# Pairs' layers of the later quarters: one fp32 matmul, or three fp32r terms of split x and split matrix

## The reference

```python
x = x + einsum('bct,bcd->bdt', x, W0[itok_B_1_198])
x = x + einsum('bct,bcd->bdt', x, W1[itok_B_0_7])
x = x + einsum('bct,bcd->bdt', x, W2[itok_B_0_7]) + bias[itok_B_0_7][:, :, None]
gate = x @ Wg + (x @ Ag[a]) @ Bg[a]          # 512 -> 2048, a = itok_B_0_7, rank 16
up   = x @ Wu + (x @ Au[a]) @ Bu[a]
h    = silu(gate) * up
x    = x + h @ Wd + (h @ Ad[a]) @ Bd[a]      # 2048 -> 512
```

## Time and profile before

| | before |
|---|---|
| median of three runs, and their range | 1240.14 us (1238.54 to 1240.18) |
| the profiled execution: its own time, its span | 1237.63 us, 1235.8 us |
| TensorE busy | 1227.7 us, 99% of the span |
| weight loads busy | 1029.7 us, 83% |
| VectorE busy | 957.1 us, 77% |
| ScalarE busy | 558.1 us, 45% |
| GpSimd busy | 710.7 us, 58% |
| granted TensorE clock | full (1.00) in the whole span |

### The profile page before, as it was taken

How to read it: one execution, slowest core, us unless ns; L and a number is a source line. 1 busy time by engine, 2 the same in 40 slices (tenths; PEclk the granted TensorE clock), 3 DMA queues, 4 the chain that set the end, 5 groups by cost and what they waited for, 6 DMA issues and landing times.

```text
span 1235.8 us, 18085 instructions
## 1 busy us (share of the span) xinstructions
PE 1227.7 (99%) x6190; PEld 1029.7 (83%) x6190; DVE 957.1 (77%) x1540; ACT 558.1 (45%) x1003; POOL 710.7 (58%) x598
## 2 busy tenths in 40 slices
PE   9999999999999999999999999999999999999998
PEld 8888888888888888888888888888888888888886
DVE  7887777887688777788678778777868877677775
ACT  4744445444544344454344444444534443444333
POOL 4676655558736556546864556555675554444453
PEclk9999999999999999999999999999999999999999
DMA  6866455556865455557496544546659442322323
GB/s 213 295 214 220 126 153 186 162 163 185 289 223 162 124 158 144 164 162 213 142 332 191 178 128 143 166 137 187 198 180 314 160 120 80 93 84 86 113 89 107
DMA packets 141690, 209.60 MB, mean 170 GB/s; under 512 B 44192, under 2 KB 88480, under 8 KB 141600
## 3 DMA queue, kind: packets, MB, share of 16 engines
q1 hardware_dynamic: 117696, 135.45, 34.8%
q0 software_dynamic: 23040, 71.85, 19.0%
q10 hardware_dynamic: 864, 1.15, 0.3%
HBM read 164.36 MB, written 44.04 MB: 169 GB/s over the span
## 4 chain that ended last, share of the span: by engine, by line
PE 97%; DVE 2%; issue 0%; ACT 0%; POOL 0%; DVEq 0%; POOLq 0%
PE px L1735 29%; PE pd L1735 28%; PE py L1735 14%; PE pz L1735 7%; PE pz L1752 3%; PE pv L1781 2%; PE pv L1779 2%; PE pd L2074 2%; PE py L1752 2%; PE px L1752 2%; PE pd L1762 1%; PE px L1886 1%; PE py L1886 1%; PE pd L1871 1%; PE px L1758 1%; PE pd L1904 0%
## 5 line engine op out<-in xcount | busy, mean ns | idle before, releaser
L803 POOL TENSOR_TENSOR h_lo<-g,h_hi 128x512 fp32r<-128x512 f32 x127 | 182.4, 1437 | 298.0 <-ACT h_hi L943 297.2
L766 POOL DMA_INDIRECT b_got<-b_table,idx_b x192 | 198.5, 1034 | 59.9 <-issue 49.9
L1735 PE MATMUL px<-xo_hi,wg_hi 128*128 128x512 f32 x516 | 207.2, 402 | 1.3 <-DVE wg_lo L1382 0.9
L1513 DVE TENSOR_TENSOR acc<-pd,acc 128x512 f32<-128x512 f32 x248 | 164.3, 684 | 51.6 <-PE pd L1735 51.6
L1382 DVE TENSOR_TENSOR wg_lo<-w_raw,wg_hi 128x512 fp32r<-128x512 f32 (+1 forms) x256 | 182.8, 720 | 26.5 <-ACT wg_hi L943 26.4
L1735 PE MATMUL px<-xo_hi,wg_lo 128*128 128x512 f32 x516 | 202.5, 392 | 0.0
L1735 PE MATMUL px<-xo_lo,wg_hi 128*128 128x512 f32 x516 | 201.0, 389 | 0.0
L943 ACT ACTIVATE wg_hi<-w_raw 128x512 fp32r<-128x512 f32 (+1 forms) x260 | 146.0, 570 | 121.1 <-PE py L1752 74.6
L1735 PE MATMUL pd<-wd_hi,h_hi 128*128 128x512 f32 x504 | 199.7, 396 | 0.0
L1735 PE MATMUL pd<-wd_lo,h_hi 128*128 128x512 f32 x504 | 197.9, 393 | 0.0
L1735 PE MATMUL pd<-wd_hi,h_lo 128*128 128x512 f32 x504 | 196.6, 390 | 0.0
(11 more groups left out here) (331 smaller groups left out, 2439.6 us busy)
## 6 DMA issues: line engine op xcount, KB each, us to landing
w_raw<-w_gu SPq DMA_DIRECT2D x65, 512.0 KB, 4.8
wd_raw<-w_dn SPq DMA_DIRECT2D x64, 256.0 KB, 3.5
xo_hi<-xops SPq DMA_DIRECT2D x21, 512.0 KB, 6.0
xo_lo<-xops SPq DMA_DIRECT2D x21, 512.0 KB, 7.3
acc<-x SPq DMA_DIRECT2D x8, 1024.0 KB, 6.8
ad_raw<-ad_table SPq DMA_DIRECT2D x16, 512.0 KB, 4.3
ad_table<-ad_rows_kept SPq DMA_DIRECT2D x12, 512.0 KB, 6.5
xops<-st_hi SPq DMA_DIRECT2D x24, 256.0 KB, 2.8
```

Source lines behind the costliest of these rows:

```text
L766: gp.indirect_dma_start(out=dst, out_offset=None, in_=rows_of, in_offset=bass.IndirectOffsetOnAxis(ap=rows.bitcast(U32), axis=0)).then_inc ...
L803: return gp.tensor_tensor(dst, src_raw, src_hi, ALU.subtract)
L1513: ins = dve.tensor_tensor(dst, pd[j][:, :], dst, ALU.add)
L1735: ins = pe.matmul(psum, w_parts[wi], x_parts[xi], start=(start and i == 0), stop=(stop and i == 2), skip_group_check=more)
```

## The change

The matrix and x of the pair are both split, and the layer becomes a `split_product`.

- ScalarE makes `x_hi`, a copy of 128x512 values: for the block's own pair in block 3 (behind `keep_s2`, and now it is ScalarE that waits for the load of x), and for the next pair right behind the bias addition that ends each layer (`add_bias`).
- GpSimd makes `x_lo`, a subtraction over 128x512: for pair 0 in block 3, behind `gather_pair`; for the next pair at the end of each block's work on GpSimd, behind `h_low(q, b, 1)` and ahead of `gather_ad`.
- VectorE makes three instructions over 128x128 of the one: `f_hi` in fp32r, `f_one` in fp32, and, behind a wait for the latter, `f_lo`, their difference, which now signals `f_done`. `f_hi` and `f_lo` lie in an unused part of `v`.
- TensorE waits for `f_done` and `x_lo_done` and issues three matmuls of 128x512.
- The memory set aside for GpSimd's transfer descriptors is 4096 bytes in each partition and not 8192, which is the room of `x_hi` and `x_lo`.

```diff
+        x_hi = sb("x_hi", [P, T], F32R)
+        x_lo = sb("x_lo", [P, T], F32R)
...
+        def pair_tokens(q, i):
+            return acc[:, (q + 1) % 2, PAIR_ORDER[i], :]
...
+        f_hi, f_lo = v[:, 1, WH:WH + P], v[:, 1, WH + P:2 * WH]
...
+            def x_low(q, i):
+                gp.wait_ge(x_hi_done, made(q, i))
+                low(x_lo[:, :], pair_tokens(q, i), x_hi[:, :]).then_inc(x_lo_done, 1)
...
                     gather_pair(q, i)
+                if pair_at(q, b) == 0:
+                    x_low(q, 0)
...
                     gather_own(q + 1, (*range(13, 16), *range(0, 2)))
+                if pair_at(q, b) is not None and pair_at(q, b + 1) is not None:
+                    x_low(q, pair_at(q, b + 1))
                 if ad_gather_at(q, b) is not None:
...
+            def x_high(q, i):
+                if i < 2:
+                    act.wait_ge(x_in[(q + 1) % 2][i], ((q + 1) // 2 + 1) * 16)
+                copy(x_hi[:, :], pair_tokens(q, i)).then_inc(x_hi_done, 1)
...
                 keep_s2(k)
+                if pair_at(q, b) == 0:
+                    x_high(q, 0)
...
-                    add_bias(acc[:, (q + 1) % 2, pair, :], pd[0][:, :], (q + 1) * QP + pair).then_inc(layer_add, 1)
+                    add_bias(pair_tokens(q, i), pd[0][:, :], (q + 1) * QP + pair).then_inc(layer_add, 1)
+                    if i + 1 < QP:
+                        x_high(q, i + 1)
...
+                    dve.tensor_tensor(f_hi, pd[2][:, 0:P], eb_one[:, i % 2, :], ALU.add)
                     dve.tensor_tensor(f_one[:, :], pd[2][:, 0:P], eb_one[:, i % 2, :], ALU.add
-                                      ).then_inc(f_done, 1)
+                                      ).then_inc(f_summed, 1)
+                    dve.wait_ge(f_summed, e)
+                    dve.tensor_tensor(f_lo, f_one[:, :], f_hi, ALU.subtract).then_inc(f_done, 1)
...
-                    if i < 2:
-                        pe.wait_ge(x_in[(q + 1) % 2][i], ((q + 1) // 2 + 1) * 16)
                     pe.wait_ge(f_done, made(q, i))
-                    pe.matmul(pd[0][:, :], f_one[:, :], acc[:, (q + 1) % 2, PAIR_ORDER[i], :],
-                              start=True, stop=True).then_inc(layer_mm, 1)
+                    pe.wait_ge(x_lo_done, made(q, i))
+                    split_product(pd[0][:, :], [f_hi, f_lo], [x_hi[:, :], x_lo[:, :]]
+                                  ).then_inc(layer_mm, 1)
...
-    nc = bacc.Bacc("TRN2", target_bir_lowering=False, num_devices=1, dynamic_dma_scratch_size=8192)
+    nc = bacc.Bacc("TRN2", target_bir_lowering=False, num_devices=1, dynamic_dma_scratch_size=4096)
```

More of the change, by code:

```diff
@@ L303, in cond_resid_kernel @@
         e_mm = sem("e_mm")
+        f_summed = sem("f_summed")
         f_done = sem("f_done")
+        x_hi_done = sem("x_hi_done")
+        x_lo_done = sem("x_lo_done")
         layer_mm = sem("layer_mm")
```

## The result

| | before | after |
|---|---|---|
| median of five runs each | 1238.62 us | 1244.66 us |
| range | 1238.09 to 1240.18 | 1244.38 to 1246.4 |
| ratio, with its 95% interval | | 1.0047 (1.0032 to 1.0062) |

The account below looks back on a forecast made before the run. TensorE bounds the kernel, 97% of the span. Gain -4.3, nine waits +9.5 and block 4's +1.2 give +6.4 us (bounds +3.9 and +8.3), on the median 1240.14 1246.5; 1244.0 to 1248.5 for this case, overall range 1239.5 to 1250.5.

Parts of the forecast that it names:

- TensorE's gain: At each of 24 layers, one fp32 matmul of 0.86 becomes three of 0.23: 0.18 gained each, 4.3 us in all.
- VectorE's own part: At the pair's matrix, `f_done` comes 0.82 behind the start of `f_hi`, 0.54 later than before, hidden by 0.94 in block 6.
- ScalarE's part: 24 copies of 128x512, 0.63 each, in ScalarE's idle time behind `add_bias`: cost nothing.
- The seam: Between `h_lo` and `x_low` at an odd block's end: VectorE's waiting sum stays held through both, its string 1.30 later.
- Rows 6: Trace at 127.72: two GpSimd subtractions back to back, 2.55 together, VectorE's sum ending behind the second; taken as more alike.
- Both rivals that let VectorE through at the seam: VectorE's string slips through, wait hidden, 1235.8 us, chance 0.12; or VectorE keeps the ports, `x_low` late, 1240.5, chance 0.12.
- rows 7: Trace at 159.38: VectorE's gate ends 0.54 behind the first of two GpSimd subtractions; taken as lower bound, 0.86 a block.
- The wait: Ahead of the layer in blocks 6, 8, 10: 1.06 us each, nine times, 9.5; first quarter's block 4: 1.2.
- The idle time in brackets: Sign to look for: about 0.9 to 1.0 of idle ahead of the layer's first matmul in blocks 6, 8 and 10.
- Block 4 of later quarters: Matrix made at 416.05; with the delays 418.33 for a layer at 418.40, just in time, so no wait.
- Odd blocks: Blocks 5, 7 and 9: `x_low` delays VectorE's work, but 2.63 of cover stand against 1.30 + 0.54, so no wait.
- The fourth case, slower gathers: GpSimd's gathers slower with half the descriptor memory, or a later load of x: +7 on top, about 1253 us, chance 0.10.

Follow-up runs that it names:

- experiment 1: The changed kernel without GpSimd's `x_low`, the layer's second term reading `x_hi` again; 0.9966 of the kernel before, 1236.06 against 1240.16 us.
- experiment 5: The changed kernel with `x_low` moved ahead of the first tile's `h_low`, all work kept; 0.9972 of the kernel before, 1234.96 against 1238.59 us.
- experiment 7: The changed kernel with the subtraction that makes `x_lo` replaced by a fill with zeros at the same place; 0.9966 of the kernel before, 1234.77 us.
- experiment 3: The kernel before with the matrix made in two parts by three VectorE instructions, the fp32 layer kept; 1.0005 of the kernel before, 1240.98 us.
- experiment 8: The changed kernel with `x_low` over 256 of the 512 columns, the other half zero; 0.9997 of the kernel before, 1237.78 us.
- experiment 9: The changed kernel with all of `x_low` done as two subtractions of 256 columns; 1.0027 of the kernel before, 1242.21 against 1238.29 us.
- experiment 6: The changed kernel with `x_low` moved ahead of the first `h_low` in odd blocks only; 0.9966 of the kernel before, 1235.07 us.
- experiment 4: The kernel before with 4096 and not 8192 bytes of descriptor memory, nothing else; 1.0007 of the kernel before, 1241.44 us.

## Why the prediction was right

The forecast was +6.4 us on the kernel before and 1246.5; measured are +6.0 and 1244.66. Of the 1.8 us between the two times, 1.5 is the median of before, which I took as 1240.14 and which is 1238.62 over five runs. That the medians differ by just 6.0 is in part luck: the interval allows 4.0 to 7.7, and the profiled executions differ by 0.9 in the opening alone, where nothing was forecast. What bears the prediction out is the stretch from 60 us on, +5.8 for +6.4, and the steps below.

- **TensorE's gain, 0.18 a layer.** 0.18 at each of 24 layers (experiments 1, 5 and 7), 4.3 in all. The layer is worth 3.8 reduced matmuls (0.86 / 0.227; the prediction divided by the rounded 0.23 and had 3.7); by the four passes of the Trainium skill ("FP8 and Floating Point Precision", TensorE Precision Notes), experiment 1 would have been 5.5 shorter from 60 us on, and it is 4.3.
- **VectorE's own part, 0.54 and hidden.** `f_lo` ends 0.81 behind the start of `f_hi` (155.94 to 156.75), 0.82 was forecast. Hidden: experiment 3.
- **ScalarE's part, nothing.** No engine but VectorE ends a wait ahead of a layer in the changed kernel, and experiment 1, which keeps the copies, has none.
- **The seam.** Rows 6 were the right pair to go by: 3.42 against 2.18, 1.24 where I had 1.30, since two subtractions back to back take 2.54 and not 2.60. Both rivals that let VectorE through at the seam are refuted in 9 of 9 blocks, and `x_lo` takes its plain 1.30 and not over 2.5. With half the size VectorE's first sum does get through (experiments 8 and 9), so the choice between rows 6 and rows 7 was a real one. The reason given for it (in rows 7 the first subtraction had itself waited) fits the full size only: in experiments 8 and 9 `h_lo` runs its plain 1.30 and VectorE gets in all the same.
- **The wait, 1.06 each.** Measured 1.01 in the nine blocks, and 1.14 for 1.2 in the first block 4. These two are the 0.5 between +6.4 and +5.9. The idle time in brackets, given as the sign to look for at 0.9 to 1.0, is 0.73: it starts 0.17 after the next matmul could have begun, which the prediction left out of the sign, though not out of the price.
- **Block 4 of later quarters, nothing.** `f_lo` is ready 0.29 before the layer there; I had 0.23, of which 0.16 for the way to TensorE. In the first quarter's block 3 `x_lo` is ready 0.22 before the layer; I had 0.4. For the block 3 the cover is thin enough that in experiment 6 it was used up.
- **Odd blocks, nothing.** `f_lo` has 1.49 or more to spare in them, although in block 5 VectorE's first sum of the next weights is held for 3.44 us, where it was 2.23.
- **The fourth case, slower gathers.** Experiment 4: none.

The Trainium skill ("SBUF — State Buffer", Who interferes with whom) has the exclusion between a VectorE instruction with two SBUF inputs and a GpSimd instruction that reads SBUF. Experiment 7 supports that it hangs on reading: the fill lets VectorE pass. Its order of issue the trace does not bear out at the full-size seam: by the recorded starts the sum was issued at 151.21, ahead of both `h_lo` (151.79) and `x_lo` (153.03), and ended behind both. GpSimd had a gather under way at 151.21 (150.83 to 151.77), but that doesn't explain it: the 186 sums of 128x256 in this trace that run beside gathers alone take 0.41 to 0.49. Why this one had not ended by 151.62, ahead of `h_lo`, the traces don't show.

## What to carry to other kernels

Before giving GpSimd one more elementwise instruction, look at which VectorE instruction stands next to it at that moment and how much cover its consumer has: the same 21 subtractions (the other three stand in block 3 in both) cost 10 us of waits at the end of a block, all of it at ten of them, and nothing when they stood ahead of an earlier `h_low`, where GpSimd had idle time. Two small delays share one cover: 0.54 on VectorE was free alone, and doubled the price of the other. For what a wait costs, take the distance of two starts, not the idle time in the bracket, which was 0.28 too small here each time.

## What the hardware showed that I had not expected

**Who gets through at a seam changes with the second instruction's size, and not by size alone.** A VectorE sum held by a GpSimd subtraction of 128x512 stays held through a second one of 128x512 (3.42 us, 9 of 9), and gets through ahead of a second one of 128x256 (2.24 us, 9 of 9 in each of two kernels). The half-size subtraction takes 1.01 in such a crossing in experiment 8, where the shortest one of experiment 9 takes 0.73, so VectorE isn't the only one that pays.

It is no rule of size in general. In each of the eleven kernels, the one before included, VectorE gets in at 24 other seams, ahead of instructions that are not small: at 12 between an `h_lo` and the 128x768 subtraction, and at 12 between that one and the next `h_lo`. At the first kind the `h_lo` had itself taken 1.61 in place of 1.30. Where the first ran its plain 1.30 and the second was of 128x512 (`x_lo` or a down weight), VectorE was held through both, in 15 of 15 cases of the changed kernel and in 3 of 3 before; but once, in the first block 3 of the changed kernel, it got in behind a plain 1.30 and ahead of the 128x512 subtraction for `ad`. No one rule for all of these came out.

**The opening varies, the rest hardly does.** From 60 us on, three kernels without a wait at a layer are 4.33, 4.40 and 4.31 shorter than before. In the first 48 us, in which no edit but the single fill at the start of experiment 8 moves an instruction, ten profiled executions (the changed kernel and nine experiments) lie between 0.0 and 4.0 us behind the one of before. Each is one execution of another kernel; that it is chance and no effect of an edit is my reading, and the 23 runs of the kernel before beside experiments 5 to 8, from 1237.68 to 1241.49, spread as much. These are windows of 10 us with each engine's busy time, TensorE first, then the granted clock; the kernel before:

```profile
10.00:20.00 10.00, 10.00 (x76) 8.75 (x75) 7.82 (x23) 2.50 (x6) 5.83 (x6) 1.00 0.76 257
20.00:30.00 10.00, 10.00 (x56) 7.18 (x55) 9.55 (x37) 8.98 (x17) 3.31 (x2) 1.00 0.73 252
```

And that of experiment 4, whose opening is 4.0 longer:

```profile
10.00:20.00 10.00, 8.38 (x74) 8.14 (x73) 5.40 (x11) 1.33 (x4) 5.95 (x6) 1.00 0.77 274
20.00:30.00 10.00, 10.00 (x38) 5.79 (x39) 8.53 (x44) 6.15 (x10) 1.26 (x2) 0.83 0.77 242
```

TensorE was idle for 1.6 us of the first window, waiting for VectorE once (1.6 us), and for 3.4 us of the next window, from 20.17 on, it was granted the lower of its two levels, 1.2 in place of 2.4 GHz. Experiment 3 has the same picture (8.38 busy, then a clock of 0.84); experiment 1 had as long a pause (8.34 busy) and kept its full clock, with an opening 2.1 longer. What makes the pause come in one execution and not in another I did not look into. It means that with one execution of each, a difference of 4 us in span says nothing in this kernel, while the part behind the opening tells 0.1 to 0.2: experiments 3 and 4, in which a layer neither gains nor waits, differ from before by 0.13 and 0.02 there, and the one stray loss seen in it is the 0.24 of experiment 6.
